# One-hot rows two chunks at a time: 192 scalar comparisons become 96 tensor comparisons in batches 1 to 3

## The reference

```python
e = jnp.stack([tbl_0[ids[:, 0]], ..., tbl_25[ids[:, 25]]], axis=1)     # 26 lookups per sample, rows of 128 floats
combined = jnp.concatenate([e, r_dense_x[:, None, :]], axis=1)         # 27 rows of 128
interact = jnp.einsum('bfd,bgd->bfg', combined, combined)
z = interact[:, _TRIU_I, _TRIU_J]                                      # the 351 pairs i < j
h = jnp.concatenate([z, r_dense_x], axis=1)                            # 479
h = jnp.maximum(h @ W_top1 + b_top1, 0.0)                              # 512
h = jnp.maximum(h @ W_top2 + b_top2, 0.0)                              # 256
y = h @ W_top3                                                         # 1
```

## Time and profile before

| | |
|---|---|
| median of 3 runs | 424.41 us (421.15 to 424.75) |
| the profiled execution, its own time | 422.81 us |
| its span in the profile | 420.7 us |
| granted TensorE clock, mean | 0.984 |
| busy: PE, PEld, POOL, DVE, ACT | 381.7, 302.6, 301.5, 210.5, 209.0 us |
| POOL's indirect DMAs | 288, 299.4 us busy, 87.9 us idle between them |
| TENSOR_SCALAR of line 606 | 192, 83.5 us busy |

### The profile page before, as it was taken

How to read it: one execution, slowest core, us unless ns; L and a number is a source line. 1 busy time by engine, 2 the same in 40 slices (tenths; PEclk the granted TensorE clock), 3 DMA queues, 4 the chain that set the end, 5 groups by cost and what they waited for, 6 DMA issues and landing times. The chain is left out here.

```text
span 420.7 us, 5912 instructions
## 1 busy us (share of the span) xinstructions
PE 381.7 (91%) x2192; PEld 302.6 (72%) x2192; DVE 210.5 (50%) x459; ACT 209.0 (50%) x347; POOL 301.5 (72%) x296
## 2 busy tenths in 40 slices
PE   1899599999998999999998999999995999996897
PEld 1677479889796766968786776968784666686696
DVE  2896749595943470926844380925823041413050
ACT  3255236665545552636455542645555255664343
POOL 7787877777877777777877777777877777777000
PEclk9999999999999999999999999999997999999899
DMA  4566743222322233221323223221111212121000
GB/s 121 157 192 186 178 118 80 70 76 76 88 76 81 52 87 88 76 76 52 94 70 80 52 79 97 74 78 50 39 50 54 54 50 58 50 57 51 14 0 2
DMA packets 16739, 32.45 MB, mean 77 GB/s; under 512 B 6387, under 2 KB 7030, under 8 KB 16712
## 3 DMA queue, kind: packets, MB, share of 16 engines
q0 software_dynamic: 9216, 18.89, 17.8%
q1 hardware_dynamic: 7496, 13.19, 10.4%
HBM read 32.05 MB, written 0.01 MB: 76 GB/s over the span
## 5 line engine op out<-in xcount | busy, mean ns | idle before, releaser
L325 POOL DMA_INDIRECT gat<-in_tbl,idx x288 | 299.4, 1040 | 87.9 <-issue 87.9
L614 DVE COPY z<-gram 32x216 f32<-32x216 f32 x128 | 49.2, 384 | 179.5 <-PE gram L391 177.2
L391 PEld LDWEIGHTS gram<-ct 128*128 128x128 f32 x1024 | 118.5, 192 | 10.9 <-issue 6.8
L391 PE MATMUL gram<-ct 128*128 128x108 f32 x1024 | 119.8, 275 | 2.2 <-ACT ct L506 1.3
L364 PE MATMUL prod<-ring,tab_hi 125*128 125x512 f32 x256 | 105.3, 411 | 13.5 <-DVE ring L600 11.0
L366 PE MATMUL prod<-ring,tab_lo 125*128 125x512 f32 x256 | 102.4, 400 | 0.0
L606 DVE TENSOR_SCALAR ring<-idb,rowid 125x512 fp32r<-125x512 int32 x192 | 83.5, 493 | 1.4
L506 ACT COPY ct<-front 128x512 f32<-128x512 f32 (+1 forms) x80 | 75.2, 1000 | 4.6 <-PE front L352 3.9
L364 PEld LDWEIGHTS prod<-ring,tab_hi 125*128 125x128 f32 x256 | 49.7, 194 | 26.4 <-issue 13.2
L514 ACT COPY z<-gram 32x216 f32<-32x216 f32 x128 | 42.1, 329 | 53.3 <-PE gram L391 52.0
L366 PEld LDWEIGHTS prod<-ring,tab_lo 125*128 125x128 f32 x256 | 49.7, 194 | 9.7
(11 more groups left out here) (63 smaller groups left out, 190.6 us busy)
## 6 DMA issues: line engine op xcount, KB each, us to landing
idb<-in_ids_t SPq DMA_DIRECT2D x24, 256.0 KB, 3.4
gat<-in_tbl,idx POOLq DMA_INDIRECT x288, 2.6
oh<-in_tbl SPq DMA_DIRECT2D x3, 500.0 KB
oh<-in_dense_t SPq DMA_DIRECT2D x4, 256.0 KB, 5.4
gat<-in_tbl SPq DMA_DIRECT2D x2, 500.0 KB
h<-in_tbl SPq DMA_DIRECT2D x2, 500.0 KB
w1z<-in_w SPq DMA_DIRECT2D x1, 702.0 KB
w2s<-in_w SPq DMA_DIRECT2D x1, 512.0 KB
```

The lines of the kernel that those rows point to most:

```text
L325: nc.gpsimd.indirect_dma_start(out=gat[:, t % GS, i, :], out_offset=None, in_=tables[f][:, :], in_offset=bass.IndirectOffsetOnAxis(ap=idx[ ...
L391: ins = nc.tensor.matmul(gram[:, c % 2, i, 0:SPG * NF].rearrange("p (j f) -> p j f", j=SPG), four.rearrange("p j f -> p (j f)"), four[:, : ...
L614: ins = nc.vector.tensor_copy(z1[QUAD * j:QUAD * (j + 1), c * CG:(c + 1) * CG, :], gram[QUAD * j:QUAD * (j + 1), c % 2, :, NF * j:NF * (j ...
```

## The change

In batches 1 to 3 a build instruction makes two neighbouring chunks. The TENSOR_SCALAR, which compares the 512 ids with one number per partition, becomes a TENSOR_TENSOR of 2 x 512 elements, whose first input is the ids read twice, and whose second is the two row numbers, each read 512 times. It waits for both chunks of the field before, and raises `built` by two. Batch 0 (line 600) stays as it is.

```diff
+KC = 2
...
+                if k % KC:
+                    return
                 if k == 0:
                     dve.wait_ge(idb_in[n % IDB], 16 * ((n - NO) // IDB + 1))
-                dve.wait_ge(used, OH_K * (n - 1) + k + 1)
-                nc.vector.tensor_scalar(ring[0:OH_P, k, :], idb[0:OH_P, n % IDB, :], rowid[0:OH_P, k:k + 1], None,
-                                        ALU.is_equal).then_inc(built, 1)
+
+                dve.wait_ge(used, OH_K * (n - 1) + k + KC)
+                nc.vector.tensor_tensor(ring[0:OH_P, k:k + KC, :],
+                                        idb[0:OH_P, n % IDB, :].unsqueeze(1).to_broadcast([OH_P, KC, SB]),
+                                        rowid[0:OH_P, k:k + KC].unsqueeze(2).to_broadcast([OH_P, KC, SB]),
+                                        ALU.is_equal).then_inc(built, KC)
```

## The result

The changed kernel takes 460.03 us (median of 4 runs, 455.23 to 463.09) against 424.58 us (4 runs): **ratio 1.080, 95% interval 1.074 to 1.087**. The forecast was 454 us, range 432 to 480. The profiled execution took 455.23 us, the shortest of the four, with a span of 453.1 us; the working gave 452.0 for that span.

What follows compares the result with a forecast made beforehand. The prediction took GpSimd's gather chain as the bound: a span of 416.4 us (the lead of 4.3 us taken off) plus 35.6 us of added holds gives 452.0, plus 2.1 outside the span 454 us; range 432 to 480.

Steps and rivals of the forecast that it cites:

- What bounds the kernel: GpSimd's chain of 288 indirect DMAs, idle only for issue gaps, binds within a few us of TensorE.
- Price on VectorE: Builds of batches 1 to 3: a pair goes from 0.80 to 1.15 us, 34 us more VectorE work in all.
- The ring: One-hot rows reach TensorE later in tiles 3, 7 and 11: 0.8 us a place, 2.4 in all, not added.
- The holds: TENSOR_TENSORs hold GpSimd's indirect DMAs 54.5 us, less 18.9 of today: last gather 35.6 us later.
- The lead at the end: In tile 15 the gathers are 4.3 us ahead of TensorE; only delay beyond that comes out at the end.
- The range: Forecast's own total 446 to 462 us: from the lower bound of delay to a slower-clock tail of some us.
- X: Delay of the last gather on GpSimd: 35.6 us, lower bound 31.
- Shut out for whole runs: Runs of TENSOR_TENSORs hold GpSimd's DMA until the run ends: delay 67.6 us, 486 us in all; chance 0.13.
- Held no more than today: New builds hold GpSimd about as much per us as now; only TensorE's delays count: 424 to 425 us; chance 0.11.
- Faster: New builds hold GpSimd not at all or under 0.20 us each, and today's 18.9 us go: 418 us; chance 0.08.

Runs made afterwards that it cites:

- tt_gram: Changed kernel with TENSOR_TENSOR pairs only between the Gram copies (44), TENSOR_SCALARs in the runs as before: 448.7 us, ratio 1.054 to the kernel before.
- tt_runs: Changed kernel with TENSOR_TENSOR pairs only in the runs behind the pair picking (52), TENSOR_SCALARs between Gram copies: 433.0 us, ratio 1.016 to the kernel before.
- extra_two: Kernel before plus 36 TENSOR_TENSORs of 125x1024 with unread output in tiles 12 to 14: 439.2 us against 421.1, no ratio given.
- ts_oneport: Kernel before with single-chunk TENSOR_SCALARs, ids laid out in three rows so VectorE cannot run two elements a cycle: 425.3 us, ratio 1.013.
- extra_one: Kernel before plus 36 TENSOR_SCALARs of 125x1023, one tensor input, unread output, in tiles 12 to 14: 422.8 us, ratio 1.009.
- few_after: Changed kernel with 13 instead of 18 gathers per tile from tile 2 on, some fields wrong: 419.6 us, ratio 0.986 to the kernel before.
- pause_again: Kernel before with a 128x1 MEMSET behind every second chunk in all runs of builds, a repeat: 617.8 us against 620.2, ratio 0.999.
- tt_single: Changed kernel with one chunk per TENSOR_TENSOR (192 of 125x512): 423.4 us, ratio 1.007 to the kernel before.

## Why the prediction was right

- **What bounds the kernel.** Right: GpSimd's unbroken chain of indirect DMAs, not the busiest engine. In before, after, tt_gram, tt_runs and extra_two the span is 31.5, 31.3, 31.5, 32.4 and 29.5 us longer than the start of the last gather, while that start moves between 389 and 422 us. (extra_two is the one in which the holds lie in the last tiles: TensorE's last wait for a gather ends 25.7 us before the last gather starts, against 20.0 us before, and the tail is 1.9 us shorter.) TensorE's wait for gathers was expected at some 30 us and is 31.4.
- **Price on VectorE.** 1226 ns taken, 1223 measured; VectorE's busy time is up 29.8 us, 34 worked out. The ring cost 4.4 us with the gathers out of the way, 2.4 worked out, and was rightly not added: no matmul of TensorE waits for it in the changed kernel.
- **The holds.** 54.5 us worked out, 49.5 measured. In the runs the working has 26 holds and 21.8 us, and 23 holds with 22.6 us were measured. Between Gram copies it has 44 holds and 32.7 us, and 37 holds with 26.9 us were measured: 0.82 us in step and not 0.87, and above all the first DMA of a group, taken at the mean of 0.52 us, came too late in its instruction to be held in 7 of 16 groups (0.27 us in the mean). The last gather was expected at 424.8 and came at 421.8.
- **The lead at the end.** This term was wrong, and that it made up for the holds was luck. I took off 4.3 us, since at the end the last gather is ahead of T4. It is as far ahead afterwards: the timeline of the changed kernel (answers to the earlier trace rows)

```profile
421.82 0.94 POOL L326 DMA_INDIRECT gat<-in_tbl,idx  x1 [0.31 <-issue]
...
427.92 0.87 PE L353 MATMUL front<-ident,gat 128*128 128x128 f32 x6
```

has 6.1 us between the two, 6.25 before. TensorE's last wait for a gather is this one, in the kernel before and in the changed one:

```profile
369.29 0.44 PE L352 MATMUL front<-ident,gat 128*128 128x128 f32 x2 [0.46 <-DMA gat<-in_tbl,idx]
```
```profile
401.75 0.44 PE L353 MATMUL front<-ident,gat 128*128 128x128 f32 x2 [0.52 <-DMA gat<-in_tbl,idx]
```

It ends 32.5 us later, and from there to the end it is 51.4 us in both. After it TensorE's own work takes longer than the gathers that are left. A lead after the last binding wait is not slack that a delay has to use up: a delay of the whole chain moves that last wait as well. Taking no lead off, and the measured 32.6 for the worked-out 35.6, gives 420.7 + 32.6 = 453.3; measured 453.1. With the measured 32.6 and the lead taken off it would have been 449.0.
- **The range.** The forecast's own range of 446 to 462 was to begin at the lower bound of 31 us for X, but 416.4 + 31 + 2.1 is 449.5; the 446 has no working behind it.
- **The rivals.** *Shut out for whole runs* did not happen in runs of TENSOR_TENSORs. *Held no more than today* would have been 424 to 425 us. *Faster* names a real effect, but not for this form: ts_oneport frees the gathers by 13.7 us and then TensorE's ring binds. The rule of the Trainium skill behind that rival (SBUF — State Buffer, the box on the "DVE blocks DMA" trap) is about the two-port mode; the other sentence of the page, in its list on the shared port pair, by which two SBUF inputs also hold a GpSimd instruction that reads SBUF, agrees with extra_two (20 of 26 DMAs held, 18.1 us), and extra_one shows that neither applies to its TENSOR_SCALARs with one tensor input (36 DMAs, none held).
- **What stays open.** The other runs of the changed kernel took 4.5 to 8 us more than the profiled one, and the median is 6 us above the forecast. Where in the instruction the first DMA of each group lands can differ between executions and would move the holds; no second trace of the same kernel was taken to show it. That holds do vary where the instructions are the same shows in batch 0 (4.6 to 9.5 us, above). The granted clock of those other runs is 0.944 to 0.952, and 0.955 in the profiled one; whether a lower clock is part of the cause or comes of longer waits is not shown.

## What to carry to other kernels

An engine whose only idle time is its own issue gap is a bound, whatever its busy share says; compare how far the start of its last instruction moves with how far the span moves. Before VectorE instructions are merged or turned into a form with two SBUF inputs, look at the length of the GpSimd-issued DMAs that start inside the existing ones: here a hold of up to 1.08 us, 0.82 in the mean of those held, and 44 instructions worth 23 us, on an engine that did not wait for VectorE once in this stretch. When two engines repeat with periods of simple ratio, take the hold of the phase that they settle in, not a mean over all phases: 0.82 us for a pair, nothing for single ones in a run.

## What the runs showed of the hardware that was not expected

- Whether a DMA gets in between two instructions depends on the form. Between TENSOR_TENSORs of 1.23 us it always did in the changed kernel (longest hold 1.08 us; few_after has two holds of 2.17 us, over more than one); in the kernel before, in runs of 16 short TENSOR_SCALARs, the third DMA waited for the end of the run (2.7 to 3.1 us, in three of three runs), though the second was let in after 0.34 us. Which one is shut out is not fixed: in the 11 such runs that VectorE went through without a wait in before, tt_gram, extra_two and extra_one it is the third in seven, the fourth in two (1.1 and 1.5 us), the second in one (4.7 us), and none in one.
- The unchanged kernel took 620 to 622 us in two sets of runs, on chips 4 and 14, and not 421 to 425 as on chips 5 and 14 before. Its granted clock was 0.82 to 0.84 there; pause_again, traced beside it, has TensorE idle behind "issue" for 65 us in the Gram matmuls. The cause is open.
- A DMA that gets in first holds VectorE in turn, by a little: in tt_single, the 37 of the 192 TENSOR_TENSORs that begin within 0.01 us of a DMA's start last 0.72 or 0.73 us, and all others 0.68 to 0.70. In a run the starts are then 0.60 to 0.61 and 0.64 to 0.65 us apart by turns, 1.25 us together like the DMAs, which fits the lockstep lasting through whole runs.
- A MEMSET of 128x1 between two instructions takes 0.06 us and does not delay the next one measurably (0.61 us from start to start in the mean, with it and without).
